# An attention and mixture-of-experts layer on one core: the experts' weights loaded in 34 pieces instead of 18, spread between a chunk's other loads

## The reference

```
x1 = x @ W1 + b1 ; x2 = x @ W2 + b2 ; z = x1 * x2
g  = z @ Wg + bg ; o = silu(g) * (z @ Wl + bl)
y  = o @ W3 + b3
```

## Time and profile before

| | before |
|---|---|
| median of the runs | 394.18 us (391.79 to 398.92) |
| the profiled execution: its time | 396.04 us |
| its span, first to last instruction | 394.2 us |
| TensorE's mean granted clock | 0.978 |
| PE busy | 357.2 us, 91% of the span |
| DMA, mean | 127 GB/s |

### The profile page before, as it was taken

One profiled execution on the slowest core, in us unless ns is written; L12 is line 12 of the kernel. 1 busy time (PEld: TensorE's weight loads), 2 busy tenths in 40 slices (PEclk: granted clock), 3 DMA queues, 4 the chain that ended last, 5 costly groups with the idle time before them and its releaser, 6 DMA issues.

```text
span 394.2 us, 15938 instructions
## 1 busy us (share of the span) xinstructions
PE 357.2 (91%) x5708; PEld 302.9 (77%) x5710; DVE 253.2 (64%) x1002; ACT 213.1 (54%) x574; POOL 219.2 (56%) x368
## 2 busy tenths in 40 slices
PE   6799899799999999999999988899999999999910
PEld 2457688688888787778888853899999999999910
DVE  4787565488886888868887765455555555555415
ACT  0577567356676665655665620655555555555400
POOL 5374644456875766667675454124666666666510
PEclk9999999899999999999999999999999999999975
DMA  7747989576769988849551002223343333333028
GB/s 200 204 134 136 175 159 157 149 98 91 190 152 164 165 183 185 192 80 153 125 138 46 19 32 61 64 84 122 126 133 118 124 124 120 121 123 116 13 60 261
DMA packets 89024, 50.23 MB, mean 127 GB/s; under 512 B 57002, under 2 KB 82252, under 8 KB 88946
## 3 DMA queue, kind: packets, MB, share of 16 engines
q1 hardware_dynamic: 85378, 43.43, 47.9%
q0 software_dynamic: 2272, 4.46, 3.5%
q10 hardware_dynamic: 1296, 1.31, 1.0%
HBM read 29.52 MB, written 11.98 MB: 105 GB/s over the span
## 4 chain that ended last, share of the span: by engine, by line
PE 81%; DVE 5%; DMA 5%; issue 3%; SPq 2%; POOL 2%; ACT 1%; ACTq 0%; POOLq 0%; DVEq 0%
PE ps L773 8%; PE ps L779 8%; PE ps L663 7%; PE ps L610 5%; PE ps L756 4%; PE ps L659 4%; PE ps L702 4%; PE ps L709 4%; PE ps L745 4%; PE ps L748 4%; PE ps L622 4%; PE ps L629 3%; PE ps L685 3%; DMA ks<-results 2%; PE ps L589 2%
## 5 line engine op out<-in xcount | busy, mean ns | idle before, releaser
L1360 POOL TENSOR_SCALAR_AFFINE_SELECT amat<-amat 128x512 f32<-128x512 f32 x64 | 41.0, 641 | 63.1 <-ACT amat L845 62.4
L1394 POOL DMA_INDIRECT results<-qas,mrowid x39 | 38.2, 980 | 66.2 <-DVE qas L1248 66.2
L858 ACT ACTIVATE pmat<-ps 128x512 f32<-128x512 f32 x64 | 38.4, 600 | 51.5 <-PE ps L663 51.5
L1161 DVE TENSOR_REDUCE mrow<-ps 128x4 f32<-128x512 f32 x64 | 43.8, 685 | 30.9 <-PE ps L610 30.9
L1230 DVE SCALAR_TENSOR_TENSOR qas<-ps,bcol,qas 128x128 f32<-128x128 f32 x78 | 26.8, 350 | 36.2 <-PE ps L779 32.4
L900 ACT ACTIVATE qas<-ps,bcol 128x128 f32<-128x128 f32 x78 | 24.4, 364 | 39.6 <-PE ps L745 39.6
L1240 DVE SCALAR_TENSOR_TENSOR qas<-ps,bcol,qas 128x128 f32<-128x128 f32 x78 | 23.9, 346 | 26.6 <-ACT qas L900 26.5
L845 ACT ACTIVATE amat<-ps 128x512 f32<-128x512 f32 x64 | 38.5, 601 | 1.9 <-DVE xscale L949 1.4
L1321 POOL DMA_INDIRECT routed<-routed_row,slot x32 | 32.6, 1018 | 10.3 <-issue 5.7
L663 PE MATMUL ps<-minus_ident,mlow 128*128 128x128 bf16 x256 | 35.5, 219 | 0.5 <-issue 0.5
L663 PE MATMUL ps<-minus_ident,mrow 128*128 128x128 bf16 x256 | 35.9, 220 | 0.0
(11 more groups left out here) (183 smaller groups left out, 930.7 us busy)
## 6 DMA issues: line engine op xcount, KB each, us to landing
kv_tok<-w SPq DMA_DIRECT2D x31, 256.0 KB
qa_parts<-wgl SPq DMA_DIRECT2D x12, 256.0 KB, 3.2
ks<-k_parts SPq DMA_DIRECT2D x32, 96.0 KB
qas<-qa_parts SPq DMA_DIRECT2D x32, 96.0 KB
xin<-routed SPq DMA_DIRECT2D x39, 72.0 KB, 1.9
ks<-k_parts SPq DMA_DIRECT2D x32, 64.0 KB
qas<-qa_parts SPq DMA_DIRECT2D x32, 64.0 KB
w<-in_W SPq DMA_DIRECT2D x4, 512.0 KB
```

The lines of the kernel that those rows point to most:

```text
L858: a_(pmat[:, u % 2].rearrange("p g t -> p (g t)"), ps[:, ST, :], ACT.Exp).then_inc(exp_done, 1)
L1161: v.tensor_reduce(mrow[:, b], ps[:, SQ, :].rearrange("p (a k) -> p a k", k=CH), AX.X, ALU.max).then_inc(max_done, 1)
L1360: q.affine_select(out=amat[:, u % 2], in_=amat[:, u % 2], compare_op=ALU.is_ge, fill=0.0, base=0, pattern=[[0, 4], [1, CH]], channel_multi ...
L1394: q.indirect_dma_start(results, bass.IndirectOffsetOnAxis(mrowid[:, m:m + 1], 0), yw[:, m, :], None, bounds_check=RESULTS - 1, oob_is_err= ...
```

## The change

The experts' weights are cut in pairs of experts in place of halves of four. That makes 34 pieces: 24 of 256 KB (W1, W2, Wg, Wl), eight of 128 KB (W3), and `b3` and `biasT` as before. The bytes, the rows of 1 KB or 512 B that they are moved in, and their places in SBUF are the same. They are issued one at a time, from chunk 4 on, at three places of every chunk's loads: ahead of the wait for `lin`, between `lin` and the wait for `win`, and behind `keys1`. The 34th goes out with chunk 15's loads.

```diff
-        N_W, N_F, N_C, N_R, N_E = 3, 4, 3, 12, 18
+        N_W, N_F, N_C, N_R, N_E = 3, 4, 3, 12, 34
...
                 if c >= 2:
+                    load_piece(c)
                     sp.wait_ge(a_ready, n + 4)
                 load_queries(c, p, 1, lin_in[p])
                 if c >= 2:
+                    load_piece(c)
                     sp.wait_ge(st_ready, n + 4)
                 load_queries(c, p, 0, win_in[p])
                 load_keys(c, p, 1, keys1_in[p])
...
-            halves = (slice(0, E // 2), slice(E // 2, E))
+            pairs = [slice(e, e + 2) for e in range(0, E, 2)]
...
-            first = NC - len(pieces) // 2 - 1
+
+            def load_piece(c):
+
+                if c >= GC and pieces:
+                    dst, src = pieces.pop(0)
+                    sp.dma_start(dst, src).then_inc(e_in, 16)
+
...
-                for dst, src in pieces[2 * (c - first):2 * (c - first) + 2] if c >= first else ():
-                    sp.dma_start(dst, src).then_inc(e_in, 16)
+                load_piece(c)
+            assert not pieces
```

More of the change, by code:

```diff
@@ L423, in _ @@
                          padrows[:].rearrange("p (a w) -> p a w", a=1).to_broadcast([CH, E, ROW])).then_inc(first_padded, 16)
-            halves = (slice(0, E // 2), slice(E // 2, E))
-            pieces = [(w12[:, h, lo:lo + F], ins[n][h].rearrange("e d f -> d e f")) for lo, n in ((0, "W1"), (F, "W2")) for h in halves] + [
+            pairs = [slice(e, e + 2) for e in range(0, E, 2)]
+            pieces = [(w12[:, h, lo:lo + F], ins[n][h].rearrange("e d f -> d e f")) for lo, n in ((0, "W1"), (F, "W2")) for h in pairs] + [
                 (wgl[:, h, k, lo:lo + F], ins[n][h, k * 128:(k + 1) * 128, :].rearrange("e d f -> d e f"))
-                for k in range(2) for lo, n in ((0, "Wg"), (F, "Wl")) for h in halves] + [
-                (w3[:, h, k, :], ins["W3"][h, k * 128:(k + 1) * 128, :].rearrange("e d f -> d e f")) for k in range(2) for h in halves] + [
+                for k in range(2) for lo, n in ((0, "Wg"), (F, "Wl")) for h in pairs] + [
+                (w3[:, h, k, :], ins["W3"][h, k * 128:(k + 1) * 128, :].rearrange("e d f -> d e f")) for k in range(2) for h in pairs] + [
                 (b3[:], split("b3")), (biasT[:], ins["biasT"].rearrange("p (e c) -> p e c", e=E))]
-            first = NC - len(pieces) // 2 - 1
+            def load_piece(c):
+                if c >= GC and pieces:
+                    dst, src = pieces.pop(0)
+                    sp.dma_start(dst, src).then_inc(e_in, 16)
             for c in range(2, NC):
```

## The result

| | before | after |
|---|---|---|
| median, 14 runs of each side by side | 395.36 us (391.79 to 404.77) | 399.61 us (395.92 to 408.18) |
| ratio | | **1.0105 [1.0067, 1.0144]** |
| the profiled execution: time, span | 396.04, 394.2 us | 397.26, 395.4 us |
| TensorE's mean granted clock | 0.978 | 0.973 |

The change makes the kernel slower, by about 1%. Forecast were 392.4 us and a range up to 398.0. A ratio here is taken over the runs within 1.5% of the fastest of their kernel; as single runs spread over some 3%, the medians of all runs stand beside it in the experiments. The change was measured twice more, with ratios of 1.0111 and 1.0070. By the medians of all runs the three measurements give 1.0107, 1.0023 and 1.0042, so the size is less firm than the sign.

The account below looks back on a forecast made before the run. TensorE (PE) was taken to set the pace from 103 to 205 us. Chunk 4 +0.3 and late code gone -2.1 make -1.8 us, from 394.18 us for the median to 392.4; range 390.0 to 398.0 us.

Parts of the forecast that it names:

- the third stage does not wait for the weights: Behind the last loads: SP waits 34.8 us for the scattered rows, and the weights land during that wait.
- The sixteen more DMAs: SP's issues: 1.5 us per chunk instead of 1.0, hidden by SP's waits in the usual chunk, otherwise 0.5 us per chunk.
- the two pieces ahead of the loads: Keys and queries queue behind two 256 KB pieces, 1.5 us against 4.5 us slack: cost 0, at most 0.1 us per chunk.
- rival C: Pieces hold up lin, win and keys1 in every chunk from 5 on, 1.4 us each, 409 us in all; chance 0.06.
- The two issue waits of the earlier trace: PE's unnamed waits of 0.50 us ahead of 156.55 and 1.60 ahead of 168.44, read as late program code.
- the one ahead of 71.44: PE's unnamed wait of 2.00 us before the pieces begin, also read as late code, with half clock for 3.5 us behind.
- the gap in q8: Instruction queue without packets for at least 6.5 and 7.1 us shortly before PE stands, taken as sign of late code.
- the gain of the bursts: Full-rate stretches of 2.5 to 3.0 us shrink to 0.73, so code comes in time: 2.1 us gained, range 0 to 2.1.
- rival A: No gain: one code wait goes and another comes, 394.2 us, or 394.5 with chunk 4's cost; chance 0.31.
- The first pieces, at chunk 4: SP comes late from the writes; pieces delay chunk 4's loads, PE waits 0 to 1.3 us once, 0.3 taken.
- The pieces' own delay: At chunk 4: two pieces delay keys1 by 1.0 us of issue plus up to 1.5 us of DMA time, at most 2.5.
- Rival B: Chunk 4 costs in earnest: PE waits 1.3 us (393.4), or late code 2.0 plus clock 1.7 without gain (397.9); chance 0.13.

Follow-up runs that it names:

- e0: The changed kernel measured again, nothing edited; ratio to before 1.0111 [1.0028, 1.0195], medians 398.64 / 397.72 us.
- h3: The changed kernel measured a third time, nothing edited; ratio to before 1.0070 [1.0037, 1.0103], median 397.85 us.
- f3: The changed kernel with 18 pieces of 512 KB at the same places; ratio to before 1.0321 [1.0251, 1.0390], medians 409.46 / 397.45 us.
- h1: The changed kernel with chunk 4's three pieces issued behind its keys1; ratio to before 1.0041 [0.9994, 1.0088], medians 398.46 / 396.17 us.
- h2: h1 with SP's wait for the writes of groups 2 and 3 moved behind chunk 4's keys1; ratio to before 0.9948 [0.9902, 0.9993], median 395.79 us.
- e1: The changed kernel with spread pieces only from chunk 6 on, W3 in halves; ratio to before 1.0029 [0.9978, 1.0080], medians 396.96 / 397.72 us.
- f4: e1 with SP's wait for the last two groups' writes moved from chunk 4 to chunk 6; ratio to before 0.9904 [0.9848, 0.9959], medians 394.89 / 397.45 us.
- g4: f4 measured again, nothing edited; ratio to before 0.9984 [0.9933, 1.0034], median 395.46 us.
- e2: The kernel before, its 18 pieces still two behind each other, but from chunk 4 on; ratio 1.0115 [1.0067, 1.0163], medians 398.83 / 397.72 us.
- g3: f4 with the last group's writes issued behind chunk 4's loads; ratio to before 1.0002 [0.9954, 1.0050], medians 394.81 / 397.28 us.
- h4: g3 measured again, nothing edited; ratio to before 0.9915 [0.9876, 0.9955], medians 393.72 / 396.17 us.
- f2: The changed kernel with no pieces in chunk 5, chunk 4's three kept, 32 pieces; ratio to before 1.0036 [0.9989, 1.0082], medians 398.95 / 397.45 us.
- e3: The kernel before with all 18 pieces issued behind chunk 15's loads; ratio to before 1.0088 [1.0044, 1.0131], medians 398.08 / 397.72 us.
- f1: The changed kernel with spread pieces from chunk 5 on, 32 pieces; ratio to before 0.9984 [0.9950, 1.0019], medians 395.21 / 397.45 us.
- g1: The kernel before with SP's wait for the last two groups' writes moved to chunk 6; ratio 0.9975 [0.9928, 1.0023], medians 395.82 / 397.28 us.
- g2: f1 with SP's wait for the last two groups' writes moved to chunk 5; ratio to before 0.9994 [0.9953, 1.0036], median 395.57 us.

## Why the prediction was wrong

**What it had right.** PE sets the pace from 103 to 205 us, and the third stage does not wait for the weights. The sixteen more DMAs and the two pieces ahead of the loads cost nothing in the usual chunk: from 97 to 205 us PE has no wait in the profile after, and in e0 and h3 none of 0.3 us that ends with a load. The pieces of f3 show that this had a limit, as rival C supposed, and that single pieces of 256 KB lie below it; of three behind one another, in h1 and h2, this is not clear. The two issue waits of the earlier trace rows and the one ahead of 71.44 are late code, as the packets show. The sign by which the forecast knew it, the gap in q8, is weaker than it looked: before has six gaps over 6 us from 50 to 205 us, and three of them have no wait of 0.3 us behind them.

By the Trainium skill's page "Runtime: NRT & Kernel Launch" (Instruction fetch mechanics), code is fetched in blocks of 256 instructions, and a crossing is mostly hidden. The spacing in the traces agrees; the waits of 0.3 to 2.0 us, at 36 of 594 crossings, are the part that is not hidden here. The fixed 2 us per DMA that rival C's sentence took from the Trainium skill's page "DMA: Bandwidth & Descriptors" (Anatomy of one DMA) is given there for DMAs that GpSimd issues; the pieces are issued by SP, and no run here singles it out for them.

**What it had half right** is the gain of the bursts. 2.1 us was forecast; the change's three profiles keep 0, 0.68 and 0.37 us of late code from 100 to 232 us, so about 1.7 is gained. But it is no rule of the size. e1, f4 and g4, as finely cut but 30 pieces from chunk 6 to the end, gain nothing: there rival A holds, one wait goes and another comes. And e2, with the pieces of before from chunk 4 on, has no such wait from 97 us on either. Why the change does better than e1, f4 and g4 is open, as is why g3 and h4, with the late writes, do (0 and 0.70).

**The step that failed** is "The first pieces, at chunk 4", priced at 0.3 us with a bound of 1.3. In the profile after, it is one wait of 2.92 us and 3.04 us lost at half clock behind it, 5.96 us. The wait was for `win`, which the step had only in brackets; it was worked out for `keys1`. Four things were missing:

- The slack came from 86.43, when PE came to chunk 4 in the profile of before. In that execution PE was late itself through its stand at 71.44. I had both rows in hand and did not join them. With PE at 84.95 as after, `win`'s slack is 0.5 us; in the 17 other profiles PE came between 83.31 and 85.58 us.
- I treated SP's start behind the writes as fixed at 75.09. In the eleven profiles in which SP waits for all of them there, it begins between 74.02 and 76.99.
- The pieces' own delay, 1.0 to 2.5 us, was too small at its upper end: from SP's first issue to the landing of `win` the change's three profiles take 1.4, 1.9 and 3.8 us more than before's 9.35.
- I charged the clock (1.7) to rival B's late code alone, not to a wait for the loads. It is the larger half of the price.

Rival B was the right case at 0.13, with its place right and its mechanism half right: the loads late, then the clock. But it had either 1.3 alone or code with 2.0 + 1.7. The range ended at that, 398.0; the price that was seen, 2.92 + 3.04 less 2.1 saved, would have given 394.2 + 3.9 = 398.1 by the prediction's own base. Of the 7.2 us between the 392.4 of the forecast and the 399.61 measured, 1.2 are that base: its three runs had a lower median than the 14 did (395.36). With that put right the forecast would still have been 393.6.

**How firmly it is shown.** Every profile of a kernel that has pieces ahead of chunk 4's `win` shows the loss, each in its one profiled execution: chunk 3 took 17.33, 17.03 and 16.06 us in the change, 17.91 in f2 and 18.14 in f3. In the thirteen others (before, e1, e2, e3, f1, f4, g1 to g4, h1, h2, h4) it took 11.37 to 15.71, 12.48 in the mean. The change's mean of 16.81 is 4.3 us above that; less 1.7 for the bursts it leaves 2.6 us, 0.7%, the lowest of the three ratios. By the times, a start at chunk 5 (f1, 0.9984 [0.9950, 1.0019]) shows none of the loss. Not settled: what else the runs with 1.0105 and 1.0111 lost, whether e2 is slower by more than its medians say, and how the loss divides between the pieces of chunks 4 and 5, since f1, f2 and h1 overlap.

## What to carry to other kernels

Take the slack of a load from an execution in which its reader was not itself held up, or take the least over several executions; a stall just ahead of a reader makes its loads look early. Where a stream of added transfers begins mattered here as much as how finely it is cut: keep it behind those loads that already come latest, and look there for a wait for a producer that covers more than these loads read. Price a stall of TensorE together with the clock behind it. A wait without a named cause can be a load or late code: look for the semaphore, or the packet of code, that came just before its end.

## What was not expected of the hardware

The clock behind a stall varied more than the stall. It was at half for some 6.8 us behind idle times of 2.92 (after), 2.62 (e0) and 1.92 + 0.53 (h3), for some 3.4 us behind 4.90 (f2), 4.99 and 2.05 (f3), 2.29 (h2), 1.99 + 0.54 (f1), 1.66 (e2), 1.50 (g2, at 160.41) and before's 2.00, and not at all behind 1.82 (e1, at 207.88), 1.60 (before, at 168.44), 1.54 (f1, at 72.49), 1.51 (h1) and 1.36 (e1). The longest stands did not have the longest slow stretch.

And how punctually the code comes late: fourteen of the 18 profiles stand for 0.3 to 2.0 us at number 1729 (about 71 us, where SP's writes end and no piece is moved yet), nine at 6081 or 6337 (159 to 168 us), four at 8385 (205 to 208 us). Which of the later blocks it is goes with the kernel: before and g1, the two with big pieces from chunk 6 on, both stand at 5825 and 6337, the seven that stand at 6081 all have pieces of 256 KB, and the four at 8385 are among the five that spread them from chunk 6 on (e1, f4, g4, h4).
